# Where beta is multiplied in a chunked delta rule: at the small inverses instead of at keys and values

## What is computed

```python
v = v * beta[..., None]
kb = k * beta[..., None]
attn = jnp.where(strict, -(kb @ sw(k)), 0.0)
T = jnp.linalg.inv(jnp.eye(chunk) - attn)
u = T @ v
w = T @ kb
def step(S, inp):                       # over the chunks
    q_i, k_i, u0, w_i = inp
    local = jnp.where(incl, q_i @ sw(k_i), 0.0)
    u_i = u0 - w_i @ S
    o_i = q_i @ S + local @ u_i
    return (S + sw(k_i) @ u_i, o_i)
```

## Time and profile before

| | us |
|---|---|
| runs (three) | 988.31, 993.73, 998.14 |
| median | 993.73 |
| profiled execution, its own time | 993.91 |
| its span, first to last instruction | 992.1 |
| TensorE busy in the span | 880.3 |
| VectorE busy | 616.4 |
| ScalarE busy | 445.0 |
| GpSimd busy | 343.2 |

### The profile page before, as it was taken

The page is one execution under the profiler, slowest core; times in us unless marked ns, Lnnn a source line. Parts: engine busy times, 40 slices in busy tenths (PEclk is TensorE's granted clock), DMA queues, the critical chain, the costliest instruction groups (busy, mean ns, idle before and its releaser), DMA issues.

```text
span 992.1 us, 18359 instructions
## 1 busy us (share of the span) xinstructions
PE 880.3 (89%) x6859; PEld 657.9 (66%) x6859; DVE 616.4 (62%) x1456; ACT 445.0 (45%) x813; POOL 343.2 (35%) x318
## 2 busy tenths in 40 slices
PE   6799789789988887899889889989998999999995
PEld 5567576667666664687556556556776777777774
DVE  5799798456888888652567776774461343333255
ACT  5687566336665554432144544445331322222221
POOL 9422201023456546332001342233540242222584
PEclk9999899768999998999799998999996999999998
DMA  5699579886545432122991112002202122221421
GB/s 166 208 271 295 167 184 267 273 221 152 107 109 116 86 59 69 54 86 103 388 376 54 63 62 79 19 23 98 80 22 82 55 65 65 65 65 49 149 64 63
DMA packets 144630, 123.53 MB, mean 125 GB/s; under 512 B 89952, under 2 KB 126752, under 8 KB 143264
## 3 DMA queue, kind: packets, MB, share of 16 engines
q1 hardware_dynamic: 141136, 112.99, 40.2%
q0 software_dynamic: 3408, 9.38, 2.5%
HBM read 74.05 MB, written 48.29 MB: 123 GB/s over the span
## 4 chain that ended last, share of the span: by engine, by line
PE 59%; DVE 16%; ACT 11%; POOL 7%; issue 4%; DMA 1%; SPq 0%; POOLq 0%; DVEq 0%; ACTq 0%
PE ps L2505 10%; PE ps L1911 5%; PE ps L2520 5%; PE ps L666 4%; DVE cross_room L1944 3%; PE ps L2369 3%; PE ps L1851 3%; PE ps L1973 2%; DVE big L1398 2%; POOL hank L345 2%; PE ps L2382 2%; PE ps L1612 2%; PE ps L423 2%; POOL kept L2652 2%; PE ps L1354 2%
## 5 line engine op out<-in xcount | busy, mean ns | idle before, releaser
L1989 ACT ACTIVATE cross_room<-ps 128x1024 f32<-128x1024 f32 x64 | 65.5, 1024 | 100.2 <-PE ps L1915 100.2
L2505 PE MATMUL ps<-wr,xbT 128*128 x312 | 101.4, 468 | 1.8 <-ACT xbT L2541 1.8
L1944 DVE TENSOR_REDUCE cross_room<-ps 128x4 f32<-128x1024 f32 x64 | 78.0, 1223 | 36.4 <-PE ps L1911 35.6
L1911 PE MATMUL ps<-kept,cross_room 32*128 32x256 f32 x512 | 75.1, 415 | 20.0 <-DVE cross_room L1944 18.5
L2594 POOL DMA_INDIRECT y_dram<-yb,dest_row x39 | 37.6, 963 | 139.4 <-DVE dest_row L2570 135.2
L2505 PEld LDWEIGHTS ps<-wr,xbT 128*128 128x128 f32 x312 | 59.9, 193 | 30.5 <-issue 4.2
L1314 POOL TENSOR_TENSOR st<-st,exponent 128x20 f32<-128x20 f32 x16 | 56.6, 3535 | 66.8 <-DVE st L1289 65.5
L1915 PE MATMUL ps<-cross_room,kept 32*128 32x256 f32 x512 | 76.2, 417 | 0.0
L1911 PEld LDWEIGHTS ps<-kept,cross_room 32*128 32x128 f32 x512 | 47.7, 193 | 38.1 <-issue 18.5
L550 DVE SCALAR_TENSOR_TENSOR room<-room 128x256 f32<-128x256 f32 x144 | 58.3, 479 | 11.3 <-ACT room L499 11.3
L2579 DVE TENSOR_TENSOR cross_room<-cross_room,ps 128x352 f32<-128x352 f32 x39 | 20.3, 521 | 61.3 <-PE ps L2505 61.3
(11 more groups left out here) (349 smaller groups left out, 2252.7 us busy)
## 6 DMA issues: line engine op xcount, KB each, us to landing
xs_dram<-params SPq DMA_DIRECT2D x17, 1040.0 KB, 17.8
room<-in_gW SPq DMA_DIRECT2D x8, 1280.0 KB, 7.8
tok_dram<-room SPq DMA_DIRECT2D x8, 768.0 KB, 6.4
fir_dram<-room SPq DMA_DIRECT2D x6, 1024.0 KB, 7.2
paths<-fir_dram SPq DMA_DIRECT2D x48, 128.0 KB, 3.7
xb<-xs_dram SPq DMA_DIRECT2D x39, 130.0 KB, 2.4
hank<-rt_dram SPq DMA_DIRECT2D x8, 512.0 KB, 7.7
yr<-y_dram SPq DMA_DIRECT2D x16, 256.0 KB, 3.6
```

The source lines that it names most:

```text
L1911: m1 = nc.tensor.matmul(ps[:, c, t * T:(t + 1) * T], strips(qS[b % 3], g, c)[:, t * P:(t + 1) * P], kS(b, g)[c * CH:(c + 1) * CH], start=T ...
L1944: V.tensor_reduce(mx[:, :, g, XD + 2 * h * CH:XD + (2 * h + 1) * CH + 1:CH].rearrange("p t c -> p c t"), ps[:, pair(h), :].rearrange("p c ...
L1989: S.activation(pT[g % 2][:, pair(h)].rearrange("p c k t -> p (c k t)"), ps[:, pair(h), :].rearrange("p c n -> p (c n)"), ACT.Exp).then_inc ...
L2505: m = nc.tensor.matmul(ps[:, 2 * (j % 2) + half, 0:FF], xbT[j % 2][:, k, :], wr[:, bass.ds(e, 1), k, half, :].rearrange("p e n -> p (e n)" ...
```

## The change

Beta is multiplied into the inverses, once, where they are made. With T the inverse, T diag(beta) replaces T, so `tok`'s own keys and values take the place of keys and values times beta in u0, u1 and w, and the product kb x k below the diagonal becomes k x k. For this:

- beta of all batches is turned by one transpose on TensorE at the last batch of the first phase, copied by ScalarE, written to a new DRAM tensor and read back as one row of 32 values per system (`sp_beta_out`, `sp_beta_in`);
- at the end of `dve_invert(g)` the transposing copy becomes a product with beta, and a second product scales the inverse in place; `sp_inverses` waits for both;
- in the second phase, L1116 and L1122, the turn of kb and its copy by ScalarE go. With them goes one sub-round of the invert stage on TensorE, ScalarE and VectorE: the turn of q and all that follows stand one sub-round earlier;
- `sp_tokens` waits for `u1_made` (L1195's piece) where it waited for `s_made` (L1188) and `vb`, since the keys and values of a batch are now read until u1 is made;
- buffers and semaphores are placed anew accordingly.

```diff
--- before.py
+++ after.py
@@ -284,6 +285,8 @@
         am = views(room3, 0, n_inv, "p (g i j) -> p g i j", g=NG, i=CH)
+        beta_rows = flat(diag[0][0:B * NP])[:, 0:P]
+        beta = flat(diag[0])[:, P:P + NG * CH].rearrange("p (g j) -> p g j", g=NG)
         no_taps = env.hank[0][0:BLK, 0, 0:SLICES * NF, :]
@@ -395,6 +398,16 @@
                               env.a_dram[b].rearrange("n c i j -> (n c) (i j)")).then_inc(*s.am_in[b // BG].up(16))
+
+        def sp_beta_out():
+            sp.wait_ge(s.beta_copied, 1)
+            nc.sync.dma_start(beta_dram.rearrange("b n q -> (b n) q"), beta_rows).then_inc(*s.beta_out.up(16))
+
+        def sp_beta_in():
+            sp.wait_ge(s.beta_out, 16)
+            for g in range(NG):
+                nc.sync.dma_start(beta[:, g], beta_dram[g * BG:(g + 1) * BG].rearrange("b n (c i) -> (b n c) i", i=CH)
+                                  ).then_inc(*s.beta_in.up(16))
 
@@ -477,6 +490,9 @@
             m.then_inc(*s.a_made.up())
+            if b == B - 1:
+                pe.wait_ge(s.beta, B)
+                nc.tensor.transpose(ps[0:B * NP, 7, 0:P], env.beta[:].rearrange("p b n -> p (b n)"), ident[:]).then_inc(*s.beta_turned.up())
             yield
@@ -533,6 +549,10 @@
             yield
+            if b == B - 1:
+                act.wait_ge(s.beta_turned, 1)
+                act.wait_ge(s.diag_out[0], 16 * B // 2)
+                S.copy(beta_rows, ps[0:B * NP, 7, 0:P]).then_inc(*s.beta_copied.up())
 
@@ -602,7 +622,7 @@
                 if k:
-                    sp.wait_ge(s.inv_step[g], 2 * (CH - 1))
+                    sp.wait_ge(s.turned[g], 2)
                 else:
@@ -641,7 +661,11 @@
             dve.wait_ge(s.inv_step[g], 2 * (CH - 1))
-            V.tensor_copy(am_, x.rearrange("p i j -> p j i")).then_inc(*s.turned[g].up())
+            dve.wait_ge(s.beta_in, 16 * NG)
+            V.tensor_tensor(am_, x.rearrange("p i j -> p j i"), beta[:, g].unsqueeze(2).broadcast_to([P, CH, CH]),
+                            ALU.mult).then_inc(*s.turned[g].up())
+            dve.wait_ge(s.turned[g], 1)
+            V.tensor_tensor(x, x, beta[:, g].unsqueeze(1).broadcast_to([P, CH, CH]), ALU.mult).then_inc(*s.turned[g].up())
             yield
@@ -656,6 +680,8 @@
                 for pair in range(PAIRS):
+                    if sl == 1 and pair == 3:
+                        pe.wait_ge(s.beta_copied, 1)
                     if sl >= 2:
@@ -740,6 +766,7 @@
         sp_triangles(B - 1)
+        sp_beta_out()
         weave([idle, pe_project, pe_normalise], B, {2: pe_filters}, {last: pe_fir()})
@@ -850,11 +877,9 @@
         x0 = early("p (n j) -> p n j", NP * CH, 2, n=NP)
-        kb = early("p (t d) -> p t d", n_x, 2, t=TT)
-        kT, kbT = early("p (c t n) -> p c t n", n_x, 2, c=KT, t=TT)
+        kT = early("p (c t n) -> p c t n", n_x, c=KT, t=TT)
         tok1 = early("p (t j d) -> p t j d", n_tok, t=TT, j=3)
         qT = early("p (c t n) -> p c t n", n_x, 2, c=KT, t=TT)
-        vb = early("p (t d) -> p t d", n_x, 2, t=TT)
         m1, m2 = early("p (n j) -> p n j", NP * CH, n=NP), early("p (n j) -> p n j", NP * DH, n=NP)
@@ -917,6 +942,8 @@
                 env.sp_late_hank(sl)
+                if sl == RING:
+                    env.sp_beta_in()
             env.sp_inverses(0)
@@ -956,15 +983,9 @@
 
-        def beta_of(b):
-            return env.beta[:, b, :].rearrange("p (t h) -> p t h", t=TT).unsqueeze(3).broadcast_to([P, TT, H, DH])
-
-
-
         def sp_tokens(b):
             i = b % 2
-            sp.wait_ge(s.s_made, b - 1)
-            sp.wait_ge(s.vb, b - 1)
+            sp.wait_ge(s.u1_made, b - 1)
             if b == 0:
@@ -1009,19 +1030,15 @@
             yield
-            pe.wait_ge(s.kb, b + 1)
-            turned(1, kb[i]).then_inc(*s.kb_turned.up())
-            yield
             pe.wait_ge(s.z, 2 * b)
...
             pe.wait_ge(s.kT, b + 1)
-            pe.wait_ge(s.kbT, b + 1)
             for t in range(TT):
...
                     for h, bank in enumerate((3, 0)):
-                        m = nc.tensor.matmul(ps[:, bank, n * P:n * P + 3 * CH], kbT[HS[h], c, t, :], kT[HS[h], c, t, 0:3 * CH],
+                        m = nc.tensor.matmul(ps[:, bank, n * P:n * P + 3 * CH], kT[HS[h], c, t, :], kT[HS[h], c, t, 0:3 * CH],
                                              start=True, stop=True)
@@ -1075,10 +1092,6 @@
             yield
-            act.wait_ge(s.kb_turned, b + 1)
-            act.wait_ge(s.a_made, b)
-            S.copy(kbT[:].rearrange("p c t n -> p (c t n)"), ps[:, 1, :]).then_inc(*s.kbT.up())
-            yield
             act.wait_ge(s.q_turned, b + 1)
@@ -1110,17 +1123,9 @@
         def dve_invert(b):
-            i, uses = b % 2, b // 2 + 1
-            dve.wait_ge(s.tok_in[i], 16 * uses)
-            dve.wait_ge(s.w_made, b - 1)
-            V.tensor_tensor(heads(kb[i][:]), heads(tok[i][:, :, 1, :]), beta_of(b), ALU.mult).then_inc(*s.kb.up())
+            i = b % 2
             for _ in range(4):
                 yield
-            dve.wait_ge(s.u1_made, b - 1)
-            if b == 0:
-                dve.wait_ge(fir.fir_made, SLICES * PAIRS)
-            V.tensor_tensor(heads(vb[i][:]), heads(tok[i][:, :, 2, :]), beta_of(b), ALU.mult).then_inc(*s.vb.up())
-            yield
             dve.wait_ge(s.l_made, b + 1)
@@ -1159,11 +1164,10 @@
                 n = t * H + c * HL + h
-                return nc.tensor.matmul(ps[HS[h], 4, c * P:(c + 1) * P], vb[i][:, t, (c * HL + h) * DH:(c * HL + h + 1) * DH],
+                return nc.tensor.matmul(ps[HS[h], 4, c * P:(c + 1) * P], tok[i][:, t, 2, (c * HL + h) * DH:(c * HL + h + 1) * DH],
                                         g0[i][:, n, :], start=True, stop=(t == 0), skip_group_check=True)
...
             yield
-            pe.wait_ge(s.vb, b + 1)
             pe.wait_ge(s.gw, 4 * b + 4)
@@ -1173,7 +1177,7 @@
                 for h in range(HL):
-                    m = nc.tensor.matmul(ps[HS[h], 5, c * P:(c + 1) * P], kb[i][:, 1, (c * HL + h) * DH:(c * HL + h + 1) * DH],
+                    m = nc.tensor.matmul(ps[HS[h], 5, c * P:(c + 1) * P], tok[i][:, 1, 1, (c * HL + h) * DH:(c * HL + h + 1) * DH],
                                          g0[i][:, H + c * HL + h, :], start=True, stop=True)
@@ -1573,8 +1577,7 @@
             for b in batches:
-                sp.wait_ge(s.s_made, B - 1)
-                sp.wait_ge(s.vb, B - 1)
+                sp.wait_ge(s.u1_made, B - 1)
                 sp.wait_ge(kv.c_turned, b - 1)
```

12 lines of the change are left out of this document (7 added, 5 removed).

## The result

| | before | after |
|---|---|---|
| runs beside each other on one chip | 4 | 4 |
| median, us | 991.02 | 996.91 |
| lowest and highest, us | 985.8, 998.14 | 993.98, 1004.66 |
| profiled execution (its span), us | 993.91 (992.1) | 993.98 (992.2) |
| mean granted clock of the profiled execution | 0.951 | 0.942 |

What follows compares the result with a forecast made beforehand. It took steady rounds as bound twice, by ScalarE and TensorE. Its terms, 2.1 - 0.45 - 0.7 + 0.5 + 3 x 1.1 + 1.15 = 5.9 us, took 993.91 to 988.0 us; range 981 to 997.

Steps and rivals of the forecast that it cites:

- the order of the steady round: Second phase: invert-stage pieces run one sub-round earlier, taking the round from 27.03 to 25.9 us, 1.1 us saved.
- late tokens: Rival: the token load (L972) lands after 12 instead of 6.5 us, delaying five rounds; +14 us, 1002; chance 0.08.
- what the row gave: ScalarE's table load in the steady round: 1.28 us for the switch, with no added drain of some 1.38 us.
- g1, 0.69, runs at 9.5 to 10.2.: TensorE's L1051 product in the steady round, timed from L1354's start; before it ran at 11.3 to 12.0.
- the clock as a rival: TensorE's granted clock around round 2: staying up gives 982.3 us, chance 0.17; one more slow stretch 993.7, chance 0.05.
- clock fallen once more: Rival: one more half-clock stretch on TensorE like round 2's, 5.7 us, giving 993.7 us; chance 0.05.
- came just before: Round 2: TensorE's 1.75 us hole, partly filled by the change, said to precede the half-clock stretch costing 5.7 us.
- Weighs the paths, 3.06, until 14.65.: VectorE's L1398 in the steady round: takes 3.06 us from 11.6, ending at 14.65 after L1354's start instead of 16.0.
- taken back: Rival: L1211 or L1138 comes 1.1 us later, steady rounds stay at 27.0, total 993 us; chance 0.20.
- The two products with beta: First phase, VectorE: two 128x1024 products at 1.2 us each replace a 1.14 us copy; first inverses leave 1.3 us later.
- l runs ahead of u1: Round 2, TensorE: L1033, 2.08 us, fits in the 1.75 us hole ahead of L1162; gain 2.1 us.
- within 1%: Whole kernel: measured time between 983.8 and 1003.7 us, chance 0.72.

Runs made afterwards that it cites:

- e1: The changed kernel with 14 extra identity transposes on TensorE in the idle gap ahead of the L1068 product, each round; median 985.48 us, ratio to before 0.9955.

## Why the prediction was wrong, step by step

**Right, to a quarter of a microsecond.** Up to g1 the order of the steady round ran as worked out. In the round from 319.55, Exp ends at t = 8.72 (forecast 8.7), the z1 copies at 9.35 (9.45), g1 starts at 9.44 (9.5), L1137 at 10.46 (10.7), without a wait for TensorE. ScalarE's hole of 2.64 us ahead of a's copies is gone, and kb with its wait too. Tokens in the steady rounds were in time:

```profile
DMA to landing us min/median/max: 4.5/6.4/16.8
```

That answers the earlier trace rows (6.5), and late tokens didn't come; only in round 2 did k's turn wait for them, 1.46 us. The table load also cost what the row gave and no more: in e1 the load takes 336.69 to 337.97 and GELU starts at 337.99; in after Exp starts 0.28 us behind its load, and that wait is for VectorE's softmax step (L1419), which I had put at t = 8.45, just where Exp then started (8.48).

**The failed step.** "g1, 0.69, runs at 9.5 to 10.2." z1 is done at t = 7.3 and the turn of u1 at 7.7, and the durations that the working used give the same, so the order I wrote down holds a hole of 1.8 us ahead of g1, in every round. The prediction doesn't mention it and gives it no price. The runs price it at 11 to 13 us for the kernel, by the clock. I had named the clock as a rival, but looked only at round 2; there "clock fallen once more" got 0.05 and one stretch, where the change makes five such holes. And I read round 2 wrongly: the hole of 1.75 us "came just before" the half clock of the earlier trace rows, I wrote. The clock had fallen already at 208.5 us, 1.1 us behind the end of an earlier hole of 1.66 us ahead of the state product. The hole of 1.75 us lay inside the slow stretch, so the trace of before had a hole of g1's size followed by a fall, but not the one that I named. Timeline of TensorE in before, then windows:

```profile
207.42 0.71 PE L1188 MATMUL ps<-kept 128*128 128x128 f32 x4 [1.66 <-ACT kept L1234]
211.50 0.70 PE L1162 MATMUL ps<-kept 128*64 128x128 f32 x4 [1.75 <-DVE kept L1262]
```

```profile
205.10:208.40 3.30, 1.64 (x16) 1.28 (x16) 1.75 (x2) 2.76 (x4) 0.18 (x1) 1.00 0.57 206
208.60:211.50 2.90, 1.15 (x13) 0.91 (x11) 2.84 (x5) 1.59 (x6) 2.90 (x1) 0.50 1.03 250
```

**A term mis-sized.** "Weighs the paths, 3.06, until 14.65." At full clock (e1) it starts at 11.37, a little ahead of the forecast 11.6, and ends at 15.54, since it takes 4.17. The 3.06 of the earlier trace rows was not the products' own time, which is 1.90, but that time and the 1.1 us that GpSimd's addition cost one of them, in an order where GpSimd's own products were all but done. The change moved VectorE's start onto GpSimd's. With it L1145, the former L1138, ends at 16.3 (15.65), the last sum at 18.4 (17.7), and from there ScalarE and TensorE took 8.5 us instead of 8.2, because a stands ahead of the logits: 26.85 instead of 25.9. So even the rival "taken back" had happened, by another cause than the ones I gave it.

**The other terms.** The two products with beta took 1.96 and 1.23 us instead of 1.2 each: the one that reads its input transposed is dearer (GpSimd did nothing at that time). A transposed read alone did not cost that much, since the copy of the earlier trace rows reads so too and took 1.14; the two products also take beta in different ways, and which of it counts wasn't tried. Timeline of VectorE after, answering:

```profile
151.71 1.96 DVE L665 TENSOR_TENSOR room<-room 128x1024 f32<-128x1024 f32 x1
153.71 1.23 DVE L668 TENSOR_TENSOR room<-room 128x1024 f32<-128x1024 f32 x1
```

In round 2, l runs ahead of u1, as forecast, but the hole before u1 is not filled, it moved; timeline of TensorE after, answering:

```profile
208.41 0.71 PE L1192 MATMUL ps<-kept 128*128 128x128 f32 x4 [1.41 <-ACT kept L1238]
209.06 1.16 PE L1050 MATMUL ps<-kept 64*128 64x128 f32 x16
212.48 0.44 PE L1167 MATMUL ps<-kept 128*64 128x128 f32 x4 [2.27 <-DVE kept L1266]
```

l takes 1.16 at full clock where it took 2.08, and the clock falls 2.3 us behind the end of the hole of 2.27 us instead, from 214.8 to 225.0. The first logits product came 2.66 us sooner than in the profile of before, against a forecast of 0.95, but over all profiles that start varies by ten, so it confirms nothing.

**The sum.** From the first to the last logits product I had forecast 4.95 us less, all of it in the first five intervals. In these five it was 1.25 less in e1, where the clock was at 1.00 throughout them, and 8.35 more as the change stands (2.3 less and 8.7 more up to the last one). 996.91 lies at the very edge of the range of 981 to 997, and "within 1%" had most of the chance; the direction was wrong all the same, by a mechanism that I had given one twentieth.
